# One-hot rows and tiles with the token column innermost, in 16 bits throughout

## What is computed

```python
def _route(tokens, router_w):
    T = tokens.shape[0]
    E = router_w.shape[0]
    capacity = int(math.ceil(T / E * CAPACITY_FACTOR))
    ...
    keep = jnp.zeros((T,), bool).at[order].set(keep_sorted)
    return jnp.where(keep, top1_idx, 0).astype(jnp.int32)
...
for e in range(E):
    h = jax.nn.relu(tokens @ W1[e] + b1[e])
    y = h @ W2[e] + b2[e]
    out = out + jnp.where((final_e == e)[:, None], y, 0.0)
```

## Time and profile before

| | |
|---|---|
| median of 3 runs | 583.29 us (582.8 to 584.12) |
| the profiled execution | 583.77 us, its span in the trace 581.6 us |
| busy over the span | PE 385.9 us (66%), DVE 402.7 us (69%), ACT 362.7 us (62%), POOL 198.0 us (34%) |
| routing's end, one-hots to `src_of` | 362.60 to 379.20 us of the span |

### The profile page before, as it was taken

How to read it: one execution, slowest core, us unless ns; L and a number is a source line. 1 busy time by engine, 2 the same in 40 slices (tenths; PEclk the granted TensorE clock), 3 DMA queues, 4 the chain that set the end, 5 groups by cost and what they waited for, 6 DMA issues and landing times.

```text
span 581.6 us, 10698 instructions
## 1 busy us (share of the span) xinstructions
PE 385.9 (66%) x2774; PEld 313.3 (54%) x2791; DVE 402.7 (69%) x1082; ACT 362.7 (62%) x831; POOL 198.0 (34%) x274
## 2 busy tenths in 40 slices
PE   0461436999999579357863321508888898888884
PEld 0320124899998434145632220407878777777874
DVE  2998994388888697669888887865555555554552
ACT  1689986577877199599934520605666665666652
POOL 7300361235445000000000000075077777777543
PEclk9999997599999779769995555766999999999999
DMA  9910000000000000002359300012011111211100
GB/s 202 267 30 0 1 0 0 2 2 1 0 0 0 1 1 0 0 0 61 88 103 270 101 0 0 1 38 47 2 50 53 53 51 52 56 52 52 36 29 33
DMA packets 34015, 25.22 MB, mean 43 GB/s; under 512 B 9096, under 2 KB 30640, under 8 KB 33968
## 3 DMA queue, kind: packets, MB, share of 16 engines
q1 hardware_dynamic: 28608, 15.17, 11.3%
q0 software_dynamic: 4096, 8.46, 5.3%
q10 hardware_dynamic: 1264, 1.03, 0.7%
HBM read 16.20 MB, written 8.45 MB: 42 GB/s over the span
## 4 chain that ended last, share of the span: by engine, by line
DVE 33%; PE 22%; issue 13%; ACT 12%; DVEq 11%; POOL 5%; DMA 3%; SPq 0%; another core or an unknown queue 0%; POOLq 0%; ACTq 0%
PE psum L912 6%; DVEq L1637 5%; PE psum L928 5%; DVE big L1486 4%; DVE feat L1382 4%; POOL out L561 3%; DVE xqT L1655 3%; DVEq L1636 3%; POOL xall L554 2%; ACT tok_b L727 2%; DMA keys<-in_ctx 2%; PE psum L920 2%; DVE feat L1645 2%; ACT big L629 2%; DVE part L1267 2%
## 5 line engine op out<-in xcount | busy, mean ns | idle before, releaser
L554 POOL DMA_INDIRECT xall<-token_rows,src_of x64 | 64.2, 1003 | 202.9 <-DVE src_of L1626 183.7
L796 ACT ACTIVATE xqT<-psum,b_now 128x128 f32<-128x128 f32 x284 | 81.0, 368 | 45.4 <-PE psum L1083 45.4
L561 POOL DMA_INDIRECT out<-xall,src_of x64 | 63.3, 990 | 50.9 <-DVE xall L1660 33.2
L1092 PE MATMUL psum<-keys,xqT 128*128 x568 | 80.1, 284 | 0.0
L1083 PE MATMUL psum<-xqT,feat 128*128 128x128 f32 x568 | 77.7, 281 | 0.0
L1083 PEld LDWEIGHTS psum<-xqT,feat 128*128 128x128 f32 x568 | 71.1, 196 | 0.0
L1092 PEld LDWEIGHTS psum<-keys,xqT 128*128 128x128 f32 x568 | 68.7, 191 | 3.5
L1655 DVE TENSOR_TENSOR xqT<-psum,keys 128x128 f32<-128x128 f32 x71 | 20.7, 292 | 69.9 <-issue 61.8
L1077 PE MATMUL psum<-ident,xqT 128*128 128x128 f32 x71 | 23.9, 336 | 35.7 <-DVE xqT L1649 31.4
L528 POOL TENSOR_TENSOR qb<-qb,arec 128x308 f32<-128x308 f32 x32 | 21.8, 700 | 72.0 <-DVE arec L1325 72.0
L784 ACT COPY xqT<-psum 128x128 f32<-128x128 f32 x71 | 18.9, 267 | 39.8 <-PE psum L1077 39.4
(11 more groups left out here) (297 smaller groups left out, 950.3 us busy)
## 6 DMA issues: line engine op xcount, KB each, us to landing
token_rows<-xall SPq DMA_DIRECT2D x4, 1040.0 KB, 8.0
xall<-in_x SPq DMA_DIRECT2D x8, 512.0 KB, 7.1
keys<-in_L_ffn_W SPq DMA_DIRECT2D x1, 2048.0 KB, 13.5
keys<-in_L_ffn_W SPq DMA_DIRECT2D x8, 256.0 KB, 6.8
keys<-in_ctx SPq DMA_DIRECT2D x4, 462.0 KB, 7.0
xall<-token_rows,src_of POOLq DMA_INDIRECT x64, 2.6
out<-xall,src_of POOLq DMA_INDIRECT x64, 2.3
big<-in_L_xattn_W_f ACTq DMA_DIRECT2D x1, 512.0 KB, 7.8
```

The lines of the kernel that those rows point to most:

```text
L554: pool.indirect_dma_start(xring[:, t % RING, :], None, rows, bass.IndirectOffsetOnAxis(ap=src_of[:, t:t + 1], axis=0)).then_inc(s_g[t % TU ...
L561: pool.indirect_dma_start(out_rows, bass.IndirectOffsetOnAxis(ap=src_of[:, t:t + 1], axis=0), yring[:, t % RING, :], None).then_inc(s_o[t ...
L796: m = act.activation(hT[a % DEPTH][:, P * c:P * c + P], bank(2 + a % 2)[:, P * c:P * c + P], ACT.Relu, bias=b1_now[a % DEPTH][:, c:c + 1])
L1092: m = pe.matmul(bank(4 + a % 2, E), hT[a % DEPTH][:, P * c:P * c + P], w2s[:, bass.ds(e, 1), c, :].rearrange("p e d -> p (e d)"), start=(c ...
```

## The change

All one-hots are laid out with the token column innermost: `hot[i]` is (tile, column) instead of (column, tile), `hot_row[i]` is (row, column), `hot_tile[i]` is (half, tile, column), each in a block of its own. The tile and row numbers of the tokens become 16-bit (`tile_b`, `row_b`), and the number tables `tile_no_b` and `row_no_b` are written out in full with each number 16 times, so that every operand of the comparisons has 16 bits and an innermost step of one. The column half of `hot_tile` is now `hot` times the full column number (`column_no_b`), one VectorE multiplication in a block; ACT keeps the partition half alone. PE has one matmul for each token column instead of two, and reads both its operands with a step of 16 elements (32 bytes) between columns. The remainders and their sums are gone: DVE makes `src_of` in two instructions instead of five.

```diff
-        tile_no_b = sb("tile_no_b", [P, TILES], BF16)
-        row_no_b = sb("row_no_b", [P, P], BF16)
+        tile_no_b = sb("tile_no_b", [P, TILES, HT], BF16)
+        row_no_b = sb("row_no_b", [P, P, HT], BF16)
+        column_no_b = sb("column_no_b", [P, B], BF16)
+        tile_b = sb("tile_b", [P, B], BF16)
+        row_b = sb("row_b", [P, B], BF16)
...
-        hot_row = xqT[:, :].rearrange("p (t r) -> p t r", t=B)
-        hot_tile = feat[:, :].bitcast(BF16)[:, 0:B * 2 * TILES].rearrange("p (t a c) -> p t a c", t=B, a=2)
-        hot = qb[:, 0:B * TILES].rearrange("p (t c) -> p t c", t=B)
+        blocks = range(B // HT)
+        hot_row = [xqT[:, i * HT * P:(i + 1) * HT * P].rearrange("p (r t) -> p r t", t=HT) for i in blocks]
+        hot_tile = [feat[:, :].bitcast(BF16)[:, i * HT * 2 * TILES:(i + 1) * HT * 2 * TILES]
+                    .rearrange("p (a c t) -> p a c t", a=2, t=HT) for i in blocks]
+        hot = [qb[:, i * HT * TILES:(i + 1) * HT * TILES].rearrange("p (c t) -> p c t", t=HT) for i in blocks]
...
                 act.wait_ge(s_ht, i + 1)
-                act.activation(hot_tile[:, i * HT:(i + 1) * HT, 0, :], hot[:, i * HT:(i + 1) * HT, :], ACT.Copy,
-                               scale=part_no[:, :])
-                for q in range(i * HT, (i + 1) * HT, QUARTER):
-                    m = act.activation(hot_tile[:, q:q + QUARTER, 1, :], hot[:, q:q + QUARTER, :], ACT.Copy,
-                                       scale=float(q // QUARTER))
-                m.then_inc(s_hp, 1)
+                act.activation(hot_tile[i][:, 0], hot[i], ACT.Copy, scale=part_no[:, :]).then_inc(s_hp, 1)
...
-                for t in range(i * HT, (i + 1) * HT):
-                    pe.matmul(bank(2, 2 * TILES), hot_row[:, t, :], hot_tile[:, t, :, :].rearrange("p a c -> p (a c)"),
-                              start=t == 0, stop=t == B - 1)
-                    n = t % QUARTER
-                    m = pe.matmul(psum[:, 3, n * TILES:(n + 1) * TILES], hot_row[:, t, :], hot[:, t, :],
-                                  start=t == 0, stop=t == B - 1)
+                for n in range(HT):
+                    m = pe.matmul(bank(2, 2 * TILES).rearrange("p (a c) -> p a c", a=2), hot_row[i][:, :, n],
+                                  hot_tile[i][:, :, :, n], start=i + n == 0, stop=i * HT + n == B - 1)
...
-            do(dve.tensor_scalar(t64[4][:, :], t64[2][:, :], MAGIC, MAGIC, ALU.add, ALU.subtract))
-            do(dve.scalar_tensor_tensor(t64[5][:, :], t64[4][:, :], -float(P), position, ALU.mult, ALU.add))
+            do(dve.tensor_scalar(tile_b[:, :], t64[2][:, :], MAGIC, MAGIC, ALU.add, ALU.subtract))
+            do(dve.scalar_tensor_tensor(row_b[:, :], tile_b[:, :], -float(P), position, ALU.mult, ALU.add))
 
             def one_hots(i):
-                t = slice(i * HT, (i + 1) * HT)
-                dve.tensor_tensor(hot[:, t, :], tile_no_b[:, :].unsqueeze(1).to_broadcast([P, HT, TILES]),
-                                  t64[4][:, t].unsqueeze(2).to_broadcast([P, HT, TILES]), ALU.is_equal
-                                  ).then_inc(s_ht, 1)
-                dve.tensor_tensor(hot_row[:, t, :], row_no_b[:, :].unsqueeze(1).to_broadcast([P, HT, P]),
-                                  t64[5][:, t].unsqueeze(2).to_broadcast([P, HT, P]), ALU.is_equal).then_inc(s_hr, 1)
+                def by_column(ap, n):
+                    return ap[:, i * HT:(i + 1) * HT].unsqueeze(1).to_broadcast([P, n, HT])
+                dve.tensor_tensor(hot[i], tile_no_b[:, :, :], by_column(tile_b, TILES), ALU.is_equal).then_inc(s_ht, 1)
+                dve.wait_ge(s_ht, i + 1)
+                dve.tensor_tensor(hot_tile[i][:, 1], hot[i], by_column(column_no_b, TILES), ALU.mult)
+                dve.tensor_tensor(hot_row[i], row_no_b[:, :, :], by_column(row_b, P), ALU.is_equal).then_inc(s_hr, 1)
...
-            w = [big[:, (14 + j) * 512:(14 + j) * 512 + TILES] for j in range(2)]
-            rest = [psum[:, 3, n * TILES:(n + 1) * TILES] for n in range(QUARTER)]
-            ch.link(dve.tensor_copy(w[0], rest[1]))
-            ch.join()
-            do(dve.scalar_tensor_tensor(w[0], rest[2], 2.0, w[0], ALU.mult, ALU.add))
-            do(dve.scalar_tensor_tensor(w[0], rest[3], 3.0, w[0], ALU.mult, ALU.add))
-            do(dve.scalar_tensor_tensor(w[1], bank(2)[:, TILES:2 * TILES], float(QUARTER), w[0], ALU.mult, ALU.add))
-            dve.scalar_tensor_tensor(src_of[:, :], w[1], float(P), bank(2)[:, 0:TILES], ALU.mult, ALU.add
+            w = big[:, 14 * 512:14 * 512 + TILES]
+            do(dve.tensor_copy(w, bank(2)[:, 0:TILES]))
+            dve.scalar_tensor_tensor(src_of[:, :], bank(2)[:, TILES:2 * TILES], float(P), w, ALU.mult, ALU.add
                                      ).then_inc(s_idx, 1)
```

More of the change, by code:

```diff
@@ L39 @@
 LAG = 17
-QUARTER = 4
 HS = G // 2
@@ L257, in xattn_moe @@
         t64 = [sb(f"t64_{n}", [P, B]) for n in range(6)]
-        t64i = [sb(f"t64i_{n}", [P, B], I32) for n in range(3)]
-        hot_row = xqT[:, :].rearrange("p (t r) -> p t r", t=B)
-        hot_tile = feat[:, :].bitcast(BF16)[:, 0:B * 2 * TILES].rearrange("p (t a c) -> p t a c", t=B, a=2)
-        hot = qb[:, 0:B * TILES].rearrange("p (t c) -> p t c", t=B)
+        blocks = range(B // HT)
[3 more added lines that the diff above has]
+        hot = [qb[:, i * HT * TILES:(i + 1) * HT * TILES].rearrange("p (c t) -> p c t", t=HT) for i in blocks]
         s_ctx = [sem(f"ctx_loaded{n}") for n in range(NP)]
@@ L504, in _ @@
                       allow_small_or_imprecise_dtypes=True).then_inc(s_const, 1)
-            pool.iota(tile_no_b[:, :], pattern=[[1, TILES]], base=0, channel_multiplier=0,
+            pool.iota(tile_no_b[:, :, :], pattern=[[1, TILES], [0, HT]], base=0, channel_multiplier=0,
                       allow_small_or_imprecise_dtypes=True).then_inc(s_const, 1)
-            pool.iota(row_no_b[:, :], pattern=[[1, P]], base=0, channel_multiplier=0,
+            pool.iota(row_no_b[:, :, :], pattern=[[1, P], [0, HT]], base=0, channel_multiplier=0,
+                      allow_small_or_imprecise_dtypes=True).then_inc(s_const, 1)
+            pool.iota(column_no_b[:, :], pattern=[[1, B]], base=0, channel_multiplier=0,
                       allow_small_or_imprecise_dtypes=True).then_inc(s_const, 1)
```

## The result

The change made the kernel slower: a median of 588.25 us over 10 runs (581.89 to 589.07) against 583.41 us (580.22 to 584.54), a ratio of 1.0087 with a 95% interval of 1.0056 to 1.0118, some 5 us. I had forecast 579.2 and a range up to 583.8. The profiled execution took 588.29 us, its span 586.5.

The account below looks back on a forecast made before the run. The bound was one narrow path from VectorE's one-hots through ACT and PE to `src_of`. PE's start -3.68, its last block +0.33 and the tail -0.78 gave -4.13 us: 579.2 us, range 577.9 to 583.8.

Parts of the forecast that it names:

- The rival of one element a cycle: VectorE's one-hots get no fast rate, so each block gains a multiplication of 1.22 us: +4.4, 587.6 us; chance 0.10.
- a factor near two: PE's matmuls on strided operands: 105 ns each in place of 56, making the last block 1.85 us.
- The strides make PE the bound: Strided reads push PE's matmuls beyond 154 ns, so all 64 follow on each other; chance 0.16.
- c = 240 ns: Cost of a load and matmul on PE with the factor 4.3: `src_of` at 381.4, kernel +2.2, 585.5 us.
- the losing end of this rival: PE's cost per matmul beyond the break-even of about 207 ns, so the kernel gets slower; chance 0.05.
- the sum: Shift of `src_of` from 379.20: PE's start -3.68, its last block +0.33, tail -0.78, together -4.13 us.
- PE's start and last block: PE's last block starts at 372.70 instead of 376.38, -3.68 us, and lasts 1.85 instead of 1.52, +0.33.
- the tail's -0.78: From PE's end to `src_of`: three VectorE instructions less, -0.78 us.
- Edits at nothing: 16-bit token numbers and POOL's larger tables cost nothing; without the cover of 47 us the tables would cost 2.4 us.
- the expectation about the sum as a shift of `src_of`: Behind `src_of`, gathers and passes move with it, so the kernel's end shifts by the same amount, -4.13 us.

Follow-up runs that it names:

- tables alone: Kernel before the change, with two unused POOL tables of 1024 and 2048 elements added: 587.07 us median against 583.35, ratio 1.0076.
- tables moved away: Changed kernel with POOL's two large tables written later, while VectorE takes the statistics of the tokens: 585.21 us median against 583.35, ratio 1.003.
- pairs run: One-hots in the old order, each token's number written twice and read as a pair, POOL's tables small: 579.04 us median, ratio 0.9936 to the kernel before.
- strided-weights run: Changed kernel with large tables written late and only PE's stationary operand at a step of 32 bytes, the moving one unbroken: single time 584.07 us.
- pairs run with added matmuls: One-hots by pairs, with 14 matmuls of 512 columns added on PE ahead of the first block: single time 578.87 us.

## Why the prediction was wrong

**VectorE.** Right in each number: durations of 0.69, 0.69 and 1.22 us, a block of 2.47, the last comparison ending 9.94 us behind the start of the first one-hot. The rival of one element a cycle did not come about.

**ACT and the tail.** Right: one instruction of 1.15 us a block, off the path; two instructions from PE's end to `src_of`.

**PE: the first step that failed.** "I take a factor near two for the forecast, 105 ns, since the row on PE itself is nearest to it." The row was of PE's output in PSUM, not of an operand that it reads. Measured were 0.239 us a matmul, 4.3 times the 56 ns that I took as the cost of unbroken columns at the high clock, and at the low clock, which it had, 2.3 times. The rival "The strides make PE the bound" is what happened, down to its size: it gave c = 240 ns and +2.2 us, and the blocks brought +2.05. The mechanism is this rival's; the close match of the size is in part luck, since its factor of 4.3 was taken on the cost at the high clock, while the pace turned out not to follow the clock and PE ran at the low one. The row that priced it, 442 ns for 64 elements in the earlier trace rows, was the nearest in form, and the chance of 0.05 for the losing end of this rival was too small. In terms of the sum: PE's start and last block, -3.68 and +0.33, became one piece of 15.5 us from the first block's comparison, +2.83 against the kernel before where the sum had -3.35; with the tail's -0.78, which came, that is the +2.05.

**POOL's tables: the second step that failed, and the dearer one.** "Edits at nothing": I named 47 us of idle time of POOL as the cover and priced its loss at 2.4 us. The two tables took 1.31 and 2.47 us in place of 0.19 and 0.24, 3.4 us more where I had 2.4, and POOL did idle; but the cover was looked for on the wrong engine. It was VectorE that paid, 3.1 us, since one of its instructions stood still while POOL wrote. Both runs on this agree: tables alone +3.7 us on the median and 2.93 in the trace, tables moved away 585.21 against the changed kernel's 588.25, -3.0.

**Behind `src_of`.** Right: the first gather, `in_pass` and the first pass (398.93 against 393.79) moved by the same 5.1 us, and nothing was taken back or added; the expectation about the sum as a shift of `src_of` holds with the sign turned.

The forecast of 579.2 us is what the pairs run reached, 579.04. The gain that the change was read to have is there on VectorE, and was given up by the layout that PE has to read and by the tables.

## What to carry to other kernels

Before a layout is turned round for one engine, look at who reads it next. Where it is TensorE's moving operand, count how many of the elements it takes one after the other lie within 16 bytes; a pair of equal numbers side by side gives VectorE the rate of 16-bit operands without turning anything. When an idle engine gets more work, check not only that engine's slack but what every other engine does during it, VectorE beside GpSimd above all, and whether GpSimd's new work stands in one queue behind other work. And where a rival's price comes from the nearest row in form (16-bit, small step, input), that row deserves more weight than one that is only on the same engine.

## What the runs showed of the hardware

GpSimd and some of VectorE's instructions hold each other up. VectorE's f32 to 16-bit subtraction, started 0.11 us after a GpSimd table, waited for it and for the next one too: 4.19 us in place of 0.70. In the run with the tables alone it started during a GpSimd `MEMSET` and waited through both tables behind it, 4.47 us. In the kernel before, GpSimd's `part_no`, a single element, started 0.02 us after VectorE's instruction and took 0.72 us; in the run with later tables, where it was ahead of VectorE, it took 0.14. The statistics of VectorE were not touched. At 0.70 us for 1056 f32 elements the subtraction runs at the fast rate of the earlier trace rows, half of 1.04 ns an element. The Trainium skill (SBUF — State Buffer, Who interferes with whom) says that VectorE in a mode that uses two ports shares one pair of them with GpSimd, and that whoever issues first blocks the other for the whole instruction; the traces agree, with the addition that two GpSimd instructions in a row held VectorE through both. No row names the mode of the subtraction; its rate fits one.

TensorE's moving operand with 2-byte elements costs 0.23 to 0.24 us for 128 columns when each column has 16 bytes or more to itself, 0.115 when two share them, and 0.108 for unbroken ones at the low clock; the first does not follow the clock, the 0.115 was seen at the low clock alone. The stationary operand, with a step of 32 bytes, leaves the pace at 0.108 at the low clock, though its load takes 164 ns in place of 142. The Trainium skill (Advanced Engine Details and Errata, SBUF Cachelines) asks for two accesses to each 16-byte line; the moving operand agrees with that, and the stationary one shows it in the length of its load but not, in these runs, in the pace of the matmuls.

The clock did not rise to 1.00 in 15.5 us in which PE was busy throughout with strided matmuls, and fell from 1.00 to 0.50 during them, while in the kernel before it rose in the second unbroken block, at about 370.7 us. Strides of the moving operand are not all there is to it: the clock also stayed at 0.50 in the four blocks of the strided-weights run, and in the pairs run with added matmuls it fell in the second block as well, with unbroken operands and PE idle between the blocks. Why, these runs do not settle.
